# Causal attention and a routed mixture of experts on one core: the experts' biases move from TensorE to GpSimd, the routing weights move from the last head group to the fourth, and the written orders of seven groups are replaced

## The reference

```python
xn = _layernorm(x, axis=-1)
# attention: 16 heads of 16, rotary embedding, causal softmax
scores = jnp.where(causal, jnp.einsum('bhnd,bhmd->bhnm', Q, K) * scale, -jnp.inf)
out = jnp.einsum('bhnm,bhmd->bhnd', jax.nn.softmax(scores, axis=-1), V)
# experts: 10 gates, 8 true experts of 256 x 256, the best two gates per token
gate_probs = jax.nn.softmax(xn @ gate_w.T + gate_b, axis=-1)
weights, selected = jax.lax.top_k(gate_probs, 2)
norm_w = true_weights / denom
expert_out = jnp.einsum('td,edh->teh', x, expert_w) + expert_b[None, :, :]
out = jnp.einsum('te,teh->th', combine_w, expert_out)
```

## Time and profile before

| what | value |
|---|---|
| median of 3 runs | 1015.39 us |
| the profiled execution's own time | 1015.35 us |
| its span | 1013.6 us |
| PE (matmul) busy | 909.3 us, 90% |
| DVE busy | 846.4 us, 83% |
| ACT busy | 727.5 us, 72% |
| POOL busy | 462.7 us, 46% |
| granted TensorE clock, mean | 0.959 of full speed |

### The profile page before, as it was taken

The page is one execution under the profiler, slowest core; times in us unless marked ns, Lnnn a source line. Parts: engine busy times, 40 slices in busy tenths (PEclk is TensorE's granted clock), DMA queues, the critical chain, the costliest instruction groups (busy, mean ns, idle before and its releaser), DMA issues. The chain is left out here.

```text
span 1013.6 us, 22104 instructions
## 1 busy us (share of the span) xinstructions
PE 909.3 (90%) x7874; PEld 389.5 (38%) x7874; DVE 846.4 (83%) x1096; ACT 727.5 (72%) x1542; POOL 462.7 (46%) x588
## 2 busy tenths in 40 slices
PE   3888445999999999999999999999999799999988
PEld 1544311333433244344443544353434233323257
DVE  6999789899889988886888788877888599994856
ACT  3556200888778888888888788878887688799922
POOL 4677659555200343344834564255222344355610
PEclk9999765899999999999999999999999899999989
DMA  9776810300200323244413542265323321022113
GB/s 324 267 256 238 285 51 6 111 2 26 68 14 2 106 85 126 78 135 145 126 54 114 151 143 76 70 167 134 82 75 118 97 60 54 23 64 64 43 42 125
DMA packets 82084, 106.65 MB, mean 105 GB/s; under 512 B 10000, under 2 KB 59064, under 8 KB 80952
## 3 DMA queue, kind: packets, MB, share of 16 engines
q1 hardware_dynamic: 74488, 85.83, 26.3%
q0 software_dynamic: 6528, 17.83, 6.7%
q10 hardware_dynamic: 960, 1.57, 0.5%
HBM read 67.37 MB, written 37.50 MB: 103 GB/s over the span
## 5 line engine op out<-in xcount | busy, mean ns | idle before, releaser
L1272 DVE TENSOR_REDUCE blk<-psP 128x2 f32<-128x1024 f32 (+2 forms) x576 | 640.9, 1161 | 102.1 <-PE psP L1415 52.0
L1218 ACT ACTIVATE probs<-psS 128x512 f32<-128x512 f32 (+3 forms) x1280 | 589.0, 540 | 163.8 <-PE psS L1455 157.9
L1455 PE MATMUL psS<-Qs,Ks 50*128 50x512 f16 (+3 forms) x1280 | 331.6, 354 | 13.4 <-ACT probs L1218 8.9
L1415 PE MATMUL psP<-Ks,Qs 48*128 48x512 f16 (+3 forms) x1280 | 295.8, 363 | 27.9 <-DVE blk L1272 17.3
L1511 PE MATMUL psO<-probs,Vs 128*32 128x512 f32 (+3 forms) x2560 | 302.7, 548 | 11.1 <-POOL probs L1119 10.1
L1119 POOL TENSOR_SCALAR_AFFINE_SELECT probs<-probs 128x512 f32<-128x512 f32 x128 | 88.1, 689 | 333.7 <-ACT probs L1218 251.3
L1455 PEld LDWEIGHTS psS<-Qs,Ks 50*128 50x128 f16 x1280 | 96.0, 93 | 252.8 <-ACT probs L1218 157.7
L1415 PEld LDWEIGHTS psP<-Ks,Qs 48*128 48x128 f16 x1280 | 80.1, 95 | 124.1 <-DVE blk L1272 90.0
L1418 PE MATMUL psP<-later,eye 64*128 64x128 bf16 x1024 | 98.3, 223 | 0.0
L1511 PEld LDWEIGHTS psO<-probs,Vs 128*32 128x32 f32 x2560 | 52.3, 109 | 93.2 <-issue 69.3
L1418 PEld LDWEIGHTS psP<-later,eye 64*128 64x128 bf16 x1024 | 75.4, 98 | 19.9 <-issue 1.7
(11 more groups left out here) (170 smaller groups left out, 724.7 us busy)
## 6 DMA issues: line engine op xcount, KB each, us to landing
xn<-we_scratch SPq DMA_DIRECT2D x72, 256.0 KB
expert_scratch<-xn SPq DMA_DIRECT2D x36, 256.0 KB, 2.6
v_scratch<-vst SPq DMA_DIRECT2D x8, 1024.0 KB, 4.0
qk_scratch<-part SPq DMA_DIRECT2D x32, 256.0 KB, 4.0
Vs<-v_scratch SPq DMA_DIRECT2D x16, 512.0 KB, 3.9
Qs<-qk_scratch SPq DMA_DIRECT2D x168, 32.0 KB
Ks<-qk_scratch SPq DMA_DIRECT2D x168, 32.0 KB
acc<-x SPq DMA_DIRECT2D x8, 512.0 KB, 9.1
```

What stands on the lines that cost most here:

```text
L1218: nc.scalar.activation(probs[u % NPR][:, h, q0:CH], psS[:, k % SB, q0:CH], ACT.Exp, scale=exp_scale).then_inc(s_read[k % SB], 1)
L1272: nc.vector.tensor_reduce(out, src, AX.X, ALU.max).then_inc(item_ok[slot], 1)
L1415: ins = pe.matmul(psP[:, slot, at:at + w], Qs[r][rows, qt // CT, p, t * P:(t + 1) * P], Ks[r][rows, kc, p, 0:w], start=True, stop=True)
L1455: pe.matmul(psS[:, k % SB, q0:CH], Ks[r][rows, kt // CT, p, kt % CT * P:(kt % CT + 1) * P], Qs[r][rows, c, p, q0:CH], start=True, stop=Tru ...
```

## The change

The bias leaves TensorE: the products of L1491, `one3` and the three-part bias are gone, the bias is kept as 32-bit numbers, and `load_e` copies an expert's row to all 128 partitions. GpSimd adds it to `yt` after ScalarE's copy, and SyncE's store waits for that addition instead of ScalarE's copy. `weights()` is called in group 3 (the fourth), behind its last `q`; `add_first()` stays. The strings "plain" and "experts" are new; "last" is not changed.

```diff
-        be_p = sb("be_p", [EXPERTS, 3, D], BF16)
...
-            step(nc.gpsimd.tensor_scalar(be_sb[:, :], be_sb[:, :], wscale[0:EXPERTS, OF_E:OF_E + 1], XSCALE, ALU.mult, ALU.mult))
-            stepped()
-            step(nc.gpsimd.tensor_copy(be_p[:, 0, :], be_sb[:, :]))
...
+            nc.gpsimd.tensor_scalar(be_sb[:, :], be_sb[:, :], wscale[0:EXPERTS, OF_E:OF_E + 1], XSCALE, ALU.mult, ALU.mult
+                                    ).then_inc(be_ok, 1)
...
-        bt = [flat[:, 10 * CH + i * D:10 * CH + (i + 1) * D] for i in range(2)]
-        one3 = sb("one3", [P, P], BF16)
+        bt = [flat[:, (13 + i) * CH:(14 + i) * CH] for i in range(2)]
...
-                    "ss10s01ssmps10ss01ss01ss01ss10spss01s01sps0s11ss0spss10s01pss01sps0s1s0s1ssp01ss01sps10sp1s0s1s0"
...
+                    "ss10s01sspms10ss1s0s10s1ss01s0sp10sss01p01ssp01sss10ps10ssp01sss10pss0s10s1sp0ss1ps0s110sspss100"
...
-                    "ss1010ssmxps01s1ss0ss10s0s1spss01s1p0ssspss011sps0ssps10s10xy1s0s01xp1s0ssp0s1ss0ys10sps1x0ss1p0"
...
+                    "1s0s1s0smsxs1s010sps0s1s0s1psss0p1s10sspss10xs01spss10y10ssps0s10sps1ss01xy01s1ss0x10ssp1ss0s01y"
...
-                    sp.dma_start(bt[buf][0:3, i * D // 2:(i + 1) * D // 2].bitcast(BF16), be_s[bass.ds(e, 1), :, :].rearrange("o p d -> (o p) d")
+                    sp.dma_start(bt[buf][:, i * D:(i + 1) * D], be_s[bass.ds(e, 1), :].to_broadcast([P, D])
                                  ).then_inc(e_in[buf], 16)
...
-                        wait_read(sp, NTH["y", EG * (g - 2) + x[1]])
+                        sp.wait_ge(y_ok, ONE + EG * (g - 2) + x[1] + 1)
...
-                            for i in range(2):
-                                nc.gpsimd.memset(bt[i], 0.0).then_inc(bt_ok, 1)
...
+                    elif x[0] == "y":
+                        n = EG * (g - 2) + x[1]
+                        wait_read(pool, NTH["y", n])
+                        pool.wait_ge(e_in[n % 2], ONE + 16 * LOADS_E * (n // 2 + 1))
+                        pool.sem_inc(carrier, 1)
+                        nc.gpsimd.tensor_tensor(yt[n % 2], yt[n % 2], bt[n % 2], ALU.add).then_inc(y_ok, 1)
...
-            nc.vector.memset(one3[:, :], 0.0).then_inc(blank, 1)
-            dve.wait_ge(blank, 4)
-            nc.vector.memset(one3[0:3, :], 1.0).then_inc(ones_ok, 1)
+            dve.wait_ge(blank, 3)
...
+                    if g == 3 and n == rest:
+                        weights()
                     if kind == "last" and n == rest:
-                        weights()
                         add_first()
...
-                    ins = pe.matmul(psS[:, bank, t * D:(t + 1) * D], one3[:, :], bt[buf][:, t * D // 2:(t + 1) * D // 2].bitcast(BF16),
-                                    start=False, stop=True)
...
-                            pe.wait_ge(ones_ok, ONE + 1)
...
-    be_s = nc.dram_tensor("be_scratch", [EXPERTS, 3, D], BF16, kind="Internal").ap()
+    be_s = nc.dram_tensor("be_scratch", [EXPERTS, D], F32, kind="Internal").ap()
```

More of the change, by code:

```diff
@@ L268, in _ @@
             sp.wait_ge(be_ok, ONE + 1)
-            sp.dma_start(be_s.rearrange("e p d -> e (p d)"), be_p[:, :, :].rearrange("e p d -> e (p d)")).then_inc(spare, 16)
+            sp.dma_start(be_s, be_sb[:, :]).then_inc(spare, 16)
             sp.wait_ge(ahead_in, ONE + 16 * 2 * LOADS)
@@ L866, in attend @@
         bout_ok = sem("bout_ok")
-        bt_ok = sem("bt_ok")
-        ones_ok = sem("ones_ok")
+        y_ok = sem("y_ok")
         added = sem("added")
@@ L924, in attend @@
             "plain": (
-                    "ss10s01ssmps10ss01ss01ss01ss10spss01s01sps0s11ss0spss10s01pss01sps0s1s0s1ssp01ss01sps10sp1s0s1s0"
-                    "sp10ssspss10s10sspms10ss10ss01ss01ps01ssp1s0ss10psss01p10sss01p0ss1s01spss1s010sspmsss1001pss10s"
-                    "s01sss01sp01sss10ps10sspsosss01ss01sp01sss10ps10ss0p1sss10psss01p01sss01psss01sss10ssps0s1s01sps"
-                    "sposs10p01sss10ps10spss10s1s0sspss01s10spmps10ss01sss01p10pssoso"),
+                    "ss10s01sspms10ss1s0s10s1ss01s0sp10sss01p01ssp01sss10ps10ssp01sss10pss0s10s1sp0ss1ps0s110sspss100"
+                    "ss1ps01ss0sss1ssmps0s10ss1s10ss0s1p0s1sp10sss01ps10s1ss0p01sss01p0s1spsss01s10sspms01ss0s1s01s1s"
+                    "0ps01ss10ssp10sss01ps10ssps01pss01s10ssp0ss1s1p0ss01spss01s10sps10ssoss10s1s0ssps01ss0ss1p0ss1sp"
+                    "1s0sposss01p10sss01p1ss0sps0s1ss10sspms0101ssspss10ss1s0pppssoos"),
             "route": "",
             "experts": (
-                    "ss1010ssmxps01s1ss0ss10s0s1spss01s1p0ssspss011sps0ssps10s10xy1s0s01xp1s0ssp0s1ss0ys10sps1x0ss1p0"
-                    "s1s01y0ss1ps01ss0sss1sspms01s0s1ss10ss01ssp01ssps1s01sp0s1s0sps1ss0pss0110xys01sps0s1s01ssxmps1s"
-                    "010sspss0s1s0s1ssps01ss10y10ss01ps10ssps0s1ssp10sss01pssos10sp01sspssx01s10sps10syss01pss01sss01"
-                    "sspss01spp1ss010yx01s10sp01sspssos10spss01psss10s01ssmyxossps10ss1s0ps1s0s1s0ppyos"),
+                    "1s0s1s0smsxs1s010sps0s1s0s1psss0p1s10sspss10xs01spss10y10ssps0s10sps1ss01xy01s1ss0x10ssp1ss0s01y"
+                    "10ssps0s1ps01ss0sss1sspms01s10ssps01ssps1s0s1p0sss01pss01sps1001ssyx10s1s0pss01sps0s1s01ssxmps1s"
+                    "0s10spss0s1s0s1sspss01s01yss01ps10sspss01ss10sp1s0ssoxs01spp10s01syss01pss01sp1s0s10spsss01ssss0"
+                    "s1p1s0sspp01ss01y1s0sps10s1sps0ssops10sx01ssps1s0s1s0spoxmyss1010sssps1s0s1s0ppyos"),
             "last": (
@@ L1064, in store_e @@
                              yt[buf].rearrange("p (t d) -> p t d", t=2)).then_inc(y_stored[buf], 16)
-            sp.wait_ge(blank, 4)
+            sp.wait_ge(blank, 3)
             for r in range(2):
@@ L1103, in _ @@
                             sp.wait_ge(ids_ok, ONE + 1)
-                            sp.wait_ge(bt_ok, ONE + 2)
                             for i in range(2):
@@ L1488, in expert @@
                         at_k, of = (2 * k + t) * P, (KC * w1 + k) * D
-                        pe.matmul(psS[:, bank, t * D:(t + 1) * D], xT[buf][:, w0, at_k:at_k + P],
-                                  wt[2 * buf + t][:, of:of + D], start=(n == 0), stop=False)
-                    ins = pe.matmul(psS[:, bank, t * D:(t + 1) * D], one3[:, :], bt[buf][:, t * D // 2:(t + 1) * D // 2].bitcast(BF16),
-                                    start=False, stop=True)
+                        ins = pe.matmul(psS[:, bank, t * D:(t + 1) * D], xT[buf][:, w0, at_k:at_k + P],
+                                        wt[2 * buf + t][:, of:of + D], start=(n == 0), stop=(n == len(todo) - 1))
                 ins.then_inc(s_ps, 1)
```

## The result

The changed kernel took 1024.42 us, the median of 3 runs (1022.56 to 1024.5), against 1015.39 us: a ratio of 1.0077, 95% interval 1.0063 to 1.0091 (the ratio is estimated over all the runs; the quotient of the two medians is 1.0089). It is slower by 9.0 us where 1007.5 us, 7.9 us faster, was forecast, and above the range (1001.5 to 1019.5).

What follows compares the result with a forecast made beforehand. At expert pairs PE, near its limit, and ScalarE were taken to stand on one chain; TensorE also stalled at seams for masks. Terms -7.85 + 0 + 6.8 - 6.85 + 0 = -7.9 us gave 1007.5 us, range 1001.5 to 1019.5.

Steps and rivals of the forecast that it cites:

- The bias off TensorE: At 36 expert pairs, two products fewer each, 72 in all: 7.85 us saved, lower end 3.9 us.
- The addition on GpSimd: At the expert pairs, 36 additions of some 1.27 us hidden, group 6's 4.84 us stall unchanged: 0 us, from 0 to +4.
- The strings: New orders of work in seven groups, priced by VectorE's idle time: 0 us, from -5 to +5.
- The weights in group 3: Seam of groups 3 and 4: chain of 6.44 us stops TensorE 4.2 us, plus 2.6 us slow clock: +6.8 us.
- The last group: add_first starts 6.44 us earlier, so the 4.25 us mask stall and its slow clock go: -6.85 us.
- rival 2: Last group: mask held later, at 953.30 or 955.78, stall some 3 us; 1013.1 us in all; chance 0.14.
- Rival 1: Last group: one of the first three masks in add_first held, about +5 us; 1019.3 us in all; chance 0.24.

Runs made afterwards that it cites:

- experiment 4: Kernel before with only the new strings "plain" and "experts", bias still as products, weights in the last group: 1012.84 us, ratio 1.0002.
- experiment 1: Changed kernel with weights() called in the last group again, nothing else: 1007.92 us, ratio 0.9952 to the kernel before.
- experiment 3: Changed kernel with the old strings and weights() in the last group, so only the bias moved: 1027.44 us, ratio 1.0151 to the kernel before.
- experiment 2: Kernel before with weights() moved to group 3 as the only edit: 1021.11 us, ratio 1.0086.
- experiment 5: Changed kernel, weights in group 3, with add_first waiting for its own result after every second instruction: 1014.87 us, ratio 1.0017 to the kernel before.
- experiment 12: Changed kernel with weights spread over group 3's second half and group 5's last pair stored before the loads, no gaps: 1007.1 us, ratio 0.9913.
- experiment 7: Changed kernel with weights in the last group and group 5's last pair stored before the 25 loads for group 7: 997.94 us, ratio 0.9856.
- experiment 9: Changed kernel with weights spread over group 3's second half, group 5's last pair stored before the loads, and gaps in add_first: 997.66 us, ratio 0.9829.
- experiment 10: Kernel before with only the store of group 5's last pair put ahead of the loads for group 7: 1008.41 us, ratio 0.9926.
- experiment 11: Kernel before with the new strings and group 5's last pair stored before the loads, bias still as products: 1009.93 us, ratio 0.9938.

## Why the prediction was wrong, point by point

**The bias off TensorE (-7.85).** Right in kind, too large. The pairs lost 0.21 us each, but groups 2 to 5 only 2.0, 1.0, 0.9 and 2.1 us (experiments 4 and 1): 6.0. The lower end of 3.9 had been set aside with the argument that ScalarE's wait is the same chain; its wait did fall by 10 us, but groups 3 and 4 gained only half of what groups 2 and 5 did. They are the groups that GpSimd fills to 65 of 105 us; that this is the cause was not shown.

**The addition on GpSimd (0, to +4).** Right with the new strings, and it would have been wrong with the old ones (experiment 3). It was priced by the sum of GpSimd's busy time and the distance to the next mask; what made masks late in experiment 3, as its traces read, is that GpSimd's queue now waits for ScalarE's copy of the pair with a split behind it. Wrong at group 6: the stall did not stay at 4.84 us but grew to 6.43 in the changed kernel and to 6.8 in experiment 1, though the store still leaves behind the loads. GpSimd's first gather, which waits for that store, starts 13.5 to 14.3 us into group 6 in the five profiles with the addition and the store behind the loads, and 11.7 to 11.9 us in the three without the addition. The cause was not tried; the profiles only show that in those five one fetch of 16 KB of instructions falls 9.1 to 9.8 us into group 6, beside that store, and in the three none does.

**The strings (0).** Right as a whole: ratio 1.0002 on their own, well inside -5 to +5 us.

**The weights in group 3 (+6.8).** The mechanism was right, the term mis-sized in two of its parts. The chain took 7.56 us and not 6.44, lengthened where GpSimd's additions run beside it (6.08 us without them, experiment 2), so TensorE stood still 5.56 us and not 4.2. And the slow clock was priced by the 5.25 us of products at 1.2 GHz in the old last group; here it was 8.41 us. The change from experiment 1 to the changed kernel is 8.6 us in group 4 and 0.7 in group 3: 9.3 us.

**The last group (-6.85).** This is the step that failed. The forecast had the held mask fall behind the end of the run, and took the masks before it as let through. In its place the fourth mask of the run was held 6.94 us. That a mask can be held at another place was rival 2, but that rival was priced at some 3 us of stall. The product behind the mask of 953.30 stood in the timeline of PE of the kernel before:

```profile
955.12 1.06 PE L1511 MATMUL psO<-probs,Vs 128*32 128x512 f32 x8
```

With the mask held to the end of the run (960.5 by the prediction) and done 0.5 us later, that is a stall of 5.9 us; TensorE waited 5.10 us. Nor was it seen that 15 us of the group's products would then run at half clock. The last group came out 3.7 us longer, not 6.9 shorter: this term alone is 10.6 us off. Experiments 5 and 12 show it: gaps in the run take the hold away and give 6 and 8.5 us.

**Sum.** With measured terms: bias 6.0 us shorter, group 6 1.5 longer, seam 9.3 longer, last group 3.7 longer, 8.5 us longer in all. The strings add 1.3 us in groups 2 to 5 (experiment 4), and what comes ahead of group 2 is 0.7 us shorter: 9.1 us, as the spans have it. All of this is from single profiles.

**The rivals.** Rival 1, on the other side, had the right sign and mechanism (a hold, +4 us in all, +5 of it in the last group against 3.7 measured) with the wrong mask: the first three of the run were let through in every profile in which it starts early. Rival 2 had the mask and not its price. The range ended at 1019.5, which is rival 1 with the seam at its upper end of 6.8; what took the result beyond it is the seam's 9.3, the bias's 6.0 instead of 7.85, and group 6.

## What to carry to other kernels

A block of work that is free where it stands (6.4 us of VectorE with 6 us of slack behind it: from the last group's first exponential to the end experiment 7 takes 125.7 us with it there, experiment 9 126.7 without it but with the gaps) is not free elsewhere at the same engine's share of busy time: look at what is queued behind it at the seam, and spread it if it must move (1.4 us instead of 9.3). Before moving work ahead of a long run of two-operand VectorE instructions, list which GpSimd instructions that run will meet; a wait in the run every second instruction lets them in. A wait at a seam that is in both profiles may be worth more than the change: one store moved ahead of 25 loads gave 7.5 us to the kernel before and 9.7 to the changed one with its weights in the last group.

## What the runs showed of the hardware that was not expected

- A GpSimd instruction can wait behind some sixteen VectorE instructions of 0.4 us, each with two operands in SBUF, until the run ends (6.94 to 7.19 us for one of 0.63). Others that meet such a run take 0.67 to 0.93 us, at most 0.30 us more than the 0.63 of one alone. At 7.42 us into the run it was held four times of four; at 6.81 us into the other run three times of seven, with the same timing ahead of it to some 10 ns. What decides is open.
- Each stall of TensorE of 3 us or more behind routing came with a granted clock of 0.50, for 3.4 to 17 us. Behind the 5.1 us stall of the last group it stayed low for 15.13 us of nearly unbroken work in the changed kernel, and for 4.2 us in experiment 2 behind the same stall, so its price cannot be taken from one row. Nor does the stall alone account for it: in experiments 10 and 11 the clock fell some 3.5 us before TensorE stopped (in experiment 10 at 953.93 us, after a stretch in which PE was busy 3.65 of 3.93 us), and it was at 0.50 without such a stall for 3.4 us in group 1 of the kernel before and 6.8 us in group 4 of experiment 11.
